# Scores of the second and third transformer layers as row sums on VectorE instead of matmuls on transposed inputs

## The reference, cut to what matters

```python
for l in range(3):
    si = x @ attn_w[l, :256]
    sj = x @ attn_w[l, 256:]
    scores = leaky(si[:, :, None] + sj[:, None, :] + attn_b[l], 0.2)
    attn = softmax(where(mask, scores, -inf))
    h = layernorm(x + attn @ x, g1[l], beta1[l])
    ff = gelu(h @ W1[l] + b1[l]) @ W2[l] + b2[l]
    x = layernorm(h + ff, g2[l], beta2[l])
```

## Time and profile before

| | us |
|---|---|
| median of 3 runs | 3887.73 |
| lowest and highest of them | 3886.62, 3899.89 |
| the profiled execution's own time | 3898.82 |
| its span, first to last instruction | 3896.9 |
| TensorE (PE) busy | 3453.9 |
| VectorE (DVE) busy | 2408.7 |
| ScalarE (ACT) busy | 2204.8 |
| GpSimd (POOL) busy | 695.6 |
| mean granted clock of TensorE | 0.946 of full |

### The profile page before, as it was taken

One profiled execution on the slowest core, in us unless ns is written; L12 is line 12 of the kernel. 1 busy time (PEld: TensorE's weight loads), 2 busy tenths in 40 slices (PEclk: granted clock), 3 DMA queues, 4 the chain that ended last, 5 costly groups with the idle time before them and its releaser, 6 DMA issues.

```text
span 3896.9 us, 60670 instructions
## 1 busy us (share of the span) xinstructions
PE 3453.9 (89%) x18816; PEld 2690.3 (69%) x18816; DVE 2408.7 (62%) x6661; ACT 2204.8 (57%) x4383; POOL 695.6 (18%) x684
## 2 busy tenths in 40 slices
PE   6789989898998989989898898989989899898976
PEld 5667767767777677777777677677767777677653
DVE  3366676666657566676666756566666666766554
ACT  2256556565564746556575564746646565565633
POOL 1211121121212111121121211112121121211110
PEclk8799999999999999999999999999999999999988
DMA  5000000000000000000000000000000000000000
GB/s 129 0 1 12 7 12 7 6 6 6 12 7 6 6 6 12 7 12 6 1 12 7 12 7 6 7 7 12 6 12 7 1 12 6 12 7 1 1 6 6
DMA packets 42354, 39.73 MB, mean 10 GB/s; under 512 B 10017, under 2 KB 40993, under 8 KB 42017
## 3 DMA queue, kind: packets, MB, share of 16 engines
q1 hardware_dynamic: 33568, 27.17, 2.4%
q0 software_dynamic: 8448, 8.39, 1.5%
HBM read 35.55 MB, written 8.39 MB: 11 GB/s over the span
## 4 chain that ended last, share of the span: by engine, by line
PE 48%; issue 33%; DVE 8%; ACT 5%; POOL 5%; DVEq 0%; DMA 0%; POOLq 0%; ACTq 0%; SPq 0%
PE acc L1188 7%; PE work L1174 7%; PE acc L1152 6%; PE work L1097 4%; PE acc L1223 4%; PE acc L1254 3%; POOL rstd L503 3%; PE acc L1235 3%; PE work L1203 2%; PE acc L1283 2%; PE work L1067 2%; PE work L1110 2%; ACT PT L1000 2%; PE work L1235 2%; PE work L1138 1%
## 5 line engine op out<-in xcount | busy, mean ns | idle before, releaser
L1174 PE MATMUL work<-XT,w_sb 128*128 128x256 f32 x3072 | 740.6, 389 | 79.6 <-ACT XT L972 60.9
L503 POOL TENSOR_TENSOR rstd<-var_eps,minus_half 128x2 f32<-128x2 f32 x320 | 233.5, 730 | 3027.9 <-DVE var_eps L727 3027.9
L1188 PE MATMUL acc<-w_sb,gT 128*128 128x256 f32 x3072 | 741.3, 389 | 0.0
L1174 PEld LDWEIGHTS work<-XT,w_sb 128*128 128x128 f32 x3072 | 565.6, 192 | 215.5 <-issue 60.1
L1188 PEld LDWEIGHTS acc<-w_sb,gT 128*128 128x128 f32 x3072 | 588.4, 196 | 101.2 <-issue 22.8
L982 ACT ACTIVATE gT<-work,b_sb 128x256 f32<-128x256 f32 x768 | 346.4, 473 | 227.0 <-PE work L1174 222.5
L1152 PE MATMUL acc<-X,PT 128*128 128x256 f32 x1536 | 359.8, 388 | 32.0 <-ACT PT L950 31.3
L1152 PEld LDWEIGHTS acc<-X,PT 128*128 128x128 f32 x1536 | 292.1, 194 | 86.9 <-issue 48.5
L711 DVE COPY PT<-work 128x512 f32<-128x512 f32 x160 | 110.2, 688 | 237.4 <-PE work L1138 234.7
L718 DVE BATCH_NORM_STATS2 stats<-R 128x6 f32<-128x256 f32 x640 | 240.9, 418 | 11.0
L1152 PE MATMUL acc<-V,PT 128*128 128x256 f32 x1024 | 234.7, 382 | 4.0 <-ACT PT L950 3.8
(11 more groups left out here) (146 smaller groups left out, 6015.0 us busy)
## 6 DMA issues: line engine op xcount, KB each, us to landing
HX<-in_x SPq DMA_DIRECT2D x16, 512.0 KB, 3.9
pos<-in_adj POOLq DMA_DIRECT2D x16, 512.0 KB, 5.5
out<-X SPq DMA_DIRECT2D x32, 256.0 KB, 2.1
w_sb<-in_L_gnn_W SPq DMA_DIRECT2D x6, 1024.0 KB, 7.9
g_sb<-in_L_gnn_g SPq DMA_DIRECT2D x6, 128.0 KB, 4.7
c_sb<-in_L_gnn_beta SPq DMA_DIRECT2D x3, 128.0 KB, 4.3
PT<-in_L_gnn_b SPq DMA_DIRECT2D x3, 128.0 KB, 5.5
beta_sb<-in_L_gnn_beta SPq DMA_DIRECT2D x1, 384.0 KB, 7.7
```

The source lines that it names most:

```text
L503: pool.tensor_tensor(rstd[s][:, half_rows(half)], var_eps[s][:, half_rows(half)], minus_half[:], ALU.pow)\
L1174: last = pe.matmul(u.bank[:, 0:HN], w1_sb[:, l, c, f * P:(f + 1) * P], XT[s][:, c, half * HN:(half + 1) * HN], start=(c == 0), stop=(c == ...
L1188: last = pe.matmul(acc[s][half][:, i, :], gT[s][:, f, i * P:(i + 1) * P], w2_sb[:, l, f, :], start=(f == 0 and i == 0), stop=(f == FC - 1) ...
```

## The change

For L1.1 and L1.2 the stages xT0, xT1 and s are gone. Two new stages, sx0 and sx1, take their place on VectorE: for each of the half's 2 tiles and each of the 2 vectors one instruction multiplies the normalised rows HX element by element with a row of `awr_sb`, writes the products to T (which nothing reads) and adds them up along the row into `s12`, starting from a constant in `ab_sb`. The factor g2 and the shift beta2 of the layer before are folded into `awr_sb` and `ab_sb` once, in the opening. Stage bc on TensorE now waits for all 8 sums. L1.0 keeps its transposes and its stage s. The new list HALF has the same other stages in another order throughout; of it the stretches around the scores are shown, the rest of it is left out.

```diff
-        ("middle", "L1.0", "f210 f211"), ("ending", "L3", "xT0"), ("ending", "L2", "sum1"),
-        ("middle", "L1.1", "xT0"), ("middle", "L1.0", "f212"), ("ending", "L3", "v0"),
-        ("ending", "L2", "norm1"), ("middle", "L1.0", "f213"), ("ending", "L3", "xT1"),
-        ("middle", "L1.0", "xsum1 xnorm1 xa1"), ("ending", "L3", "load qk0"), ("middle", "L1.1", "xT1"),
-        ("ending", "L3", "sq0"), ("middle", "L1.1", "s bc"), ("ending", "L3", "sr0"), ("middle", "L1.1", "zs0"),
...
+        ("middle", "L1.0", "xsum0 xnorm0"), ("ending", "L3", "xT0"), ("middle", "L1.0", "xa0"),
+        ("ending", "L2", "sum1"), ("middle", "L1.0", "f210 f211"), ("ending", "L3", "v0"),
+        ("middle", "L1.1", "sx0"), ("middle", "L1.0", "f212 f213"), ("ending", "L2", "norm1"),
+        ("ending", "L3", "xT1"), ("middle", "L1.0", "xsum1"), ("ending", "L3", "load"),
+        ("middle", "L1.0", "xnorm1 xa1"), ("ending", "L3", "qk0"), ("middle", "L1.1", "sx1"),
+        ("ending", "L3", "sq0 sr0"), ("middle", "L1.1", "bc zs0"), ("ending", "L3", "v1"),
+        ("middle", "L1.1", "mx0 zs1 exp0 mx1"), ("ending", "L3", "qk1"), ("middle", "L1.1", "exp1 pT0 pT1"),
+        ("ending", "L3", "ex0 ex1 sq1 ex2"), ("middle", "L1.1", "agg0"), ("ending", "L3", "ex3 sr1"),
...
+        ("middle", "L1.1", "xnorm1 xa1"), ("ending", "L3", "rr1 rt0 uT28 uT29 uT30 uT31"),
+        ("middle", "L1.2", "sx1"), ("ending", "L3", "rb0 rt1 rb1"), ("middle", "L1.2", "bc zs0"),
+        ("ending", "L3", "hn0"), ("middle", "L1.2", "mx0 zs1"), ("ending", "L3", "proj0 pv3"),
+        ("middle", "L1.2", "exp0 mx1"), ("ending", "L3", "hn1"), ("middle", "L1.2", "exp1 pT0"),
...
-        aw_sb = sb("aw_sb", [P, L, DC, 2])
+
+        aw_sb = sb("aw_sb", [P, DC, 2])
+        awr_sb = sb("awr_sb", [P, L - 1, 2, D])
...
-            uses += [(f"xT0 {k}", DC), (f"xT1 {k}", DC), (f"s {k}", 1), (f"bc {k}", 1), (f"pT {k}", NT)]
+            uses += [(f"xT0 {k}", DC), (f"xT1 {k}", DC), (f"s {k}", 1)] if k == L1K[0] else []
+            uses += [(f"bc {k}", 1), (f"pT {k}", NT)]
...
+        scored = signal("scored", [(k, 2 * NT) for k in L1K[1:]])
...
-        N_LOADS = {"L0": 3, "L2": 2 + 4} | {k: 2 * DC + 1 + 7 + 4 for k in L1K}
-        N_LOADS[L1K[0]] += 1
+        N_LOADS = {"L0": 3, "L2": 2 + 4} | {k: 2 + 5 + 4 for k in L1K}
+        N_LOADS[L1K[0]] += 2 * DC
         N_CONSTS = 8
-        N_FOLDED = {"L0": 2 * DC + 1, "L2": 2 * DC} | {k: 4 for k in L1K}
+        N_FOLDED = {"L0": 2 * DC + 1, "L2": 2 * DC} | {L1K[0]: 4} | {k: 7 for k in L1K[1:]}
...
-                for half in range(2):
-                    for c in range(DC):
-                        load(key, aw_sb[:, l, c, half:half + 1],
-                             attn_w[l, half * D + c * P:half * D + (c + 1) * P].rearrange("(p one) -> p one", one=1))
+                if l == 0:
+                    for half in range(2):
+                        for c in range(DC):
+                            load(key, aw_sb[:, c, half:half + 1],
+                                 attn_w[l, half * D + c * P:half * D + (c + 1) * P].rearrange("(p one) -> p one", one=1))
+                else:
+                    load(key, awr_sb[:, l - 1].rearrange("p k d -> p (k d)"), attn_w[l:l + 1, :].broadcast_to([P, 2 * D]))
...
-                load_columns(key, g2t_sb[:, l], g2[l])
-                load_columns(key, beta2t_sb[:, l], beta2[l])
...
+                        row = awr_sb[:, l - 1]
+                        shifts = PT2[:, 1, 3, 2 * P - 2 * l:2 * P - 2 * l + 2]
+                        dve.tensor_scalar(row[:, 0], row[:, 0], -1.0, None, ALU.mult).then_inc(folded[key], 1)
+                        dve.wait_ge(folded[key], 2)
+                        hold(dve)
+                        for k in range(2):
+                            dve.tensor_tensor_reduce(PT2[:, 2 + k, l - 1, :], row[:, k], beta2_sb[:, l - 1], 1.0, 0.0, ALU.mult, ALU.add,
+                                                     shifts[:, k:k + 1]).then_inc(folded[key], 1)
+                        dve.wait_ge(folded[key], 4)
+                        dve.tensor_tensor(row, row, g2_sb[:, l - 1:l].broadcast_to([P, 2, D]), ALU.mult).then_inc(folded[key], 1)
+                        dve.tensor_tensor(ab_sb[:, l, :, 0], shifts[:, 0:1].broadcast_to([P, NT]), bias, ALU.subtract)\
+                            .then_inc(folded[key], 1)
+                        dve.tensor_copy(ab_sb[:, l, :, 1], shifts[:, 1:2].broadcast_to([P, NT])).then_inc(folded[key], 1)
                     dve.wait_ge(folded[key], N_FOLDED[key])
...
-                    if key in L1K[1:]:
-                        l = L1K.index(key) - 1
-                        dve.tensor_scalar(there, here, g2t_sb[:, l, 1:2], beta2t_sb[:, l, 1:2], ALU.mult, ALU.add)\
-                            .then_inc(u.evacuated, 1)
-                    else:
-                        dve.tensor_copy(there, here).then_inc(u.evacuated, 1)
+                    dve.tensor_copy(there, here).then_inc(u.evacuated, 1)
...
+            def scores_of_rows(half):
+                def stage(s, it, key):
+
+                    l = L1K.index(key)
+                    dve.wait_ge(normed.sems[s], normed.value(it, L1K[l - 1] + " x", half))
+                    hold(dve)
+                    for t in tiles(half):
+                        for k in range(2):
+                            dve.tensor_tensor_reduce(T[s][:, t, k * D:(k + 1) * D], HX[s][:, t, :], awr_sb[:, l - 1, k], 1.0,
+                                                     ab_sb[:, l, t, k:k + 1], ALU.mult, ALU.add, s12[s][:, t, k:k + 1])\
+                                .then_inc(scored.sems[s], 1)
+                return stage
...
-                    if key in L1K[1:]:
-                        l = L1K.index(key) - 1
-                        act.activation(there, here, ACT.Identity, scale=g2t_sb[:, l, 0:1], bias=beta2t_sb[:, l, 0:1])\
-                            .then_inc(u.evacuated, 1)
-                    else:
-                        act.activation(there, here, ACT.Copy).then_inc(u.evacuated, 1)
+                    act.activation(there, here, ACT.Copy).then_inc(u.evacuated, 1)
...
-                    elif key in L1K[1:]:
-                        pe.wait_ge(normed.sems[s], normed.value(it, L1K[L1K.index(key) - 1] + " x", half))
-                        transpose_tiles(s, it, f"xT{half} {key}", HX[s], tiles(half))
...
-                if key in L1K:
+                if key == L1K[0]:
                     u = Use(s, it, f"s {key}")
                     pe.wait_ge(u.evacuated, u.turn + 1)
+                elif key in L1K:
+                    pe.wait_ge(scored.sems[s], scored.value(it, key, 2 * NT - 1))
```

More of the change, by code:

```diff
@@ L181, in build @@
         beta1t_sb = sb("beta1t_sb", [P, L, DC])
-        g2t_sb = sb("g2t_sb", [P, L, DC])
-        beta2t_sb = sb("beta2t_sb", [P, L, DC])
         g1_sb = sb("g1_sb", [P, L, D])
@@ L591, in wait_weights @@
                     dve.tensor_tensor(c1_sb[:, l], c1_sb[:, l], PT2[:, 1, l, 0:D], ALU.add).then_inc(folded[key], 1)
-                    dve.tensor_scalar(aw_sb[:, l, :, 0], aw_sb[:, l, :, 0], -1.0, None, ALU.mult).then_inc(folded[key], 1)
-                    dve.memset(ab_sb[:, l], 0.0).then_inc(folded[key], 1)
-                    dve.wait_ge(folded[key], 3)
-                    dve.tensor_scalar(ab_sb[:, l, :, 0], PT2[:, 1, 3, l:l + 1].broadcast_to([P, NT]), -1.0, None, ALU.mult)\
-                        .then_inc(folded[key], 1)
+                    bias = PT2[:, 1, 3, l:l + 1].broadcast_to([P, NT])
+                    if l == 0:
+                        dve.tensor_scalar(aw_sb[:, :, 0], aw_sb[:, :, 0], -1.0, None, ALU.mult).then_inc(folded[key], 1)
+                        dve.memset(ab_sb[:, l], 0.0).then_inc(folded[key], 1)
+                        dve.wait_ge(folded[key], 3)
+                        dve.tensor_scalar(ab_sb[:, l, :, 0], bias, -1.0, None, ALU.mult).then_inc(folded[key], 1)
+                    else:
+                        row = awr_sb[:, l - 1]
[11 more added lines that the diff above has]
+                        dve.tensor_copy(ab_sb[:, l, :, 1], shifts[:, 1:2].broadcast_to([P, NT])).then_inc(folded[key], 1)
                     dve.wait_ge(folded[key], N_FOLDED[key])
@@ L875, in _ @@
             stages = {"masks": make_masks, "xT": x_transposed(None), "xT0": x_transposed(0), "xT1": x_transposed(1),
-                      "s": scores_of_x, "mx0": leaky_relu(0), "mx1": leaky_relu(1),
+                      "s": scores_of_x, "sx0": scores_of_rows(0), "sx1": scores_of_rows(1), "mx0": leaky_relu(0), "mx1": leaky_relu(1),
                       "sum0": aggregated(0), "sum1": aggregated(1), "norm0": norm(0), "norm1": norm(1),
@@ L1110, in scores_of_x @@
                         last = pe.matmul(u.bank[:, 2 * t:2 * t + 2], XT[s][:, c, t * P:(t + 1) * P],
-                                         aw_sb[:, L1K.index(key), c, :], start=(c == 0), stop=(c == DC - 1))
```

(5 more changed lines are left out.)

## The result

The changed kernel took **3977.38 us** (median of 4 runs, 3970.7 to 3978.74), the kernel before beside it 3890.34: a ratio of 1.0216, with a 95% interval of 1.0194 to 1.0239. It is slower by 2.2%. The forecast said 3776, faster.

The account below looks back on a forecast made before the run. TensorE was taken as the bound, 91% busy where two graphs overlap. A step gains 3.9 + 3.15 - 0.8 + 0.9 = 7.1 us, fifteen 107, with the opening 112: 3787, as a median 3776; range about 3710 to 3880.

Parts of the forecast that it names:

- What VectorE gets: VectorE, per graph: 16 row sums at 0.33 us added, copies and additions removed, net +2.9 us; 0.8 a step exposed.
- signs of being wrong: Half clock behind both broadcasts, waits for line 732 or transpose copies up over 2 us a step, sums much above 0.33.
- L1.1, work on TensorE: Scores of L1.1: first half's transposes give 0.43 us; the broadcast starts at 1033.0 instead of 1035.11, 2.1 us gained.
- L1.1, the clock: Behind L1.1's score matmuls: the half clock goes with them, 1.8 us a step, all of it taken.
- the 3.9 forecast: From qk0 to pv0 at L1.1: 2.1 us from the earlier broadcast and 1.8 us from the clock.
- 0.43 + 0.9 = 1.3 us: L1.2 on TensorE: 0.43 us from the first half's transposes, 0.9 from the small matmul starting earlier.
- half of 2.7: Half clock behind L1.2's scores: 1.9 us at the projection, 0.8 at the small matmul; the middle, 1.35 a step, taken.
- the last ending at 0.50: Row of the last graph's ending: no score matmul runs, yet the clock is 0.50 from 3878.6 to 3885.2 at the projection.
- The new order: The new list puts other work into the waits that arise: 0.9 us a step gained, at most 1.8.
- The opening: First graph alone: shorter latency to the broadcast gives 7.6 us over two layers; less the longer fold, net gain 5.
- The clock still falls: Rival: short waits replace the matmuls and the half clock stays; 3.1 us a step gained, 3837 us, chance 0.21.
- The rival on the slow side: Sums delay VectorE's queue by all 5.3 us, one more clock fall costs 2.7: 4.1 a step lost, 3944, chance 0.07.

Follow-up runs that it names:

- GpSimd late: GpSimd's second-half scaling and X1 shift wait until the next layer's leaky relus are done: sums in old order 3862.94 us, changed kernel 3913.21, kernel before 3924.07.
- GpSimd behind the sums: The changed kernel, with GpSimd's scaling of a half waiting until VectorE has summed that half's rows: 4012.08 us, ratio 1.0306.
- the sums without GpSimd's work: Sums in the old order, GpSimd's scaling and shifting of layer outputs and X1 shift cut to 4 columns: 3833.13 us; kernel before with the same cut 3898.35.

## Why the prediction was wrong

**The step that failed** is "What VectorE gets": "Four row sums at 0.33 us end at 1032.7" and "I take 0.8" for what is exposed. The price was taken from the fold's sums, which run in the opening; it said what a sum costs alone, and not what it costs beside GpSimd. At L1.1 four of them take 5.16 us in the place shown, and TensorE waits 3.56 us for them, where it was to start 2.1 us earlier. Undisturbed they take 1.69 us, for which 1.3 were forecast; a price well above 0.33 us stood among the prediction's own signs of being wrong.

The runs divide the 2.2% into parts, by ratios to the kernel before. The collision costs 1.6% in either order (1.0056 to 1.0216 in the new one, 0.9911 to 1.0069 in the old one), and the new order costs 1.45 or 1.47% with sums (0.9911 to 1.0056 with GpSimd late, 1.0069 to 1.0216 as it was). What is left, the sums in the old order with GpSimd late, is the gain of 0.9%. These three sum to the 2.16% by construction; what supports them is that the collision and the order's price each came out alike on both ways. Neither the gain nor the order's price is clean, though. The gain is measured against a kernel in which GpSimd isn't late; against the matmuls with GpSimd's work in the same place it is 1.5% (late) and 1.7% (left out). And a collision is left in the new order even with GpSimd late, at L1.2 (below).

**The row that would have told it** was in the trace before. Line 651 is a row reduction with both inputs in SBUF, like the new sums, and line 826 the same instruction with one input in PSUM. Durations of line 651 in the kernel before:

```profile
L651 DVE CUSTOM_DVE_ANT_0 T<-T,pos x256: 676/687/1537, 24.7 to 3707.1; 128x512 f32<-128x512 f32 x128
```

And of line 826, the half of it that reads the work banks:

```profile
L826 DVE CUSTOM_DVE_ANT_0 T<-work,pos x128: 685/686/693, 330.3 to 3861.2; 128x512 f32<-128x512 f32 x128
```

The first has a maximum of 1537 over a median of 687, the second varies by 8 ns, and not for want of company: of all 512 instructions of line 826, 98 ran for over 0.3 us beside one of GpSimd's scalings or shifts, and took 681 to 693 ns like the others. A long one of line 651, in the timeline of the kernel before:

```profile
1152.63 1.27 POOL L513 TENSOR_TENSOR R<-R,c_sb 128x512 f32<-128x512 f32 x1
1153.04 1.41 DVE L651 CUSTOM_DVE_ANT_0 T<-T,pos 128x512 f32<-128x512 f32 x1
```

It ends 0.55 us after GpSimd's: most of its own 0.68 comes only then. In the kernel before VectorE's copies for the scores read PSUM (line 627) and took 546 ns at most, 535 in the middle. The change swapped an instruction that no GpSimd instruction stretched for one that it holds, and put it where GpSimd is busy by construction. The Trainium skill says this outright (SBUF — State Buffer, section "SBUF: two separate sides"): VectorE and GpSimd share a port pair as an exclusive lock, held for the whole instruction, and a VectorE instruction with two SBUF inputs needs it against a GpSimd instruction that reads SBUF. The traces agree for GpSimd's scaling and shifting, 0.48 against up to 2.55 us; for its `rstd` instruction, which reads SBUF too, only in part. It gets longer behind a running sum (0.96 us for 0.70), but it is shown as busy beside two further sums and holds neither; there the measurement decides. The prediction weighed the page on the clock and missed this one.

**L1.1, work on TensorE: right when undisturbed.** The forecast was that the broadcast comes 2.1 us earlier; with GpSimd late, in the old order, it came 8.42 - 6.08 = 2.3 earlier. But what follows it gained less: v1 then waited 1.52 us for VectorE's head scores, which is the next thing late. "An engine that waits for something else" had to be asked once more behind the broadcast.

**L1.1, the clock: right in kind.** With the sums undisturbed in the old order, the half clock from qk0 to pv0 is gone (4.9 to 0.0), so it belonged to the score work or to what stood around it; with 2 of the 16 matmuls left it was 2.0. As the change was made, it grew to 8.5, and TensorE's wait of 3.56 us stands ahead of it. In the kernel with GpSimd behind the sums, 5.0 us at half stand ahead of the broadcast, behind a wait of 2.83 us for normalised rows. This much agrees with the Trainium skill (TensorE: Matmul & The Clock Gate, Part 1: The HAM clock gate), by which idle time brings the clock down; that score matmuls with 0.26 us of waiting did the same isn't what it would lead one to expect. But even undisturbed the segment from the broadcast to pv0 is hardly shorter than before (30.84 and 29.86 against 30.20): the 1.8 us did not come through there. The new wait for the head scores takes 1.52 us of them; what takes the rest was not looked for. The mean clock, forecast near 0.955, was 0.938 in the changed kernel and 0.954 with GpSimd late in the old order. From qk0 to pv0 the gain was 1.7 us (GpSimd late) and 2.7 (its work left out) of the 3.9 forecast.

**L1.2: right in its work, wrong in its clock.** 0.43 + 0.9 = 1.3 us were forecast up to the broadcast; from pv0 to it the step became 1.6 shorter with the sums in the old order and GpSimd late. Of the clock I took half of 2.7. At the projection, 1.9 of the 2.7, almost nothing came: it takes 3.78 us as in the earlier trace rows. The small matmul takes 1.12 in place of the 1.70 of the earlier trace rows, but in 8 of 14 steps it took 1.12 before as well, so that its 0.8 was read from one of the slow places. The timeline of TensorE after:

```profile
1379.03 1.12 PE L1292 MATMUL work<-T,head_rows 4*128 4x512 f32 x2 [0.68 <-ACT T L1047]
1380.08 0.95 PE L1143 MATMUL work<-ident,s 128*128 128x128 f32 x4
1381.90 3.78 PE L1300 MATMUL acc<-wo_sb,XT 128*128 128x256 f32 x8 [0.87 <-DVE XT L879]
```

The row that spoke against it, the last ending at 0.50, was the better witness.

**The new order: wrong in sign.** I took 0.9 us a step gained; with the matmuls it costs 1.95, with undisturbed sums 3.4. A part of it is seen: with GpSimd late the first half's sums of L1.2 still took 1.11 and 1.48 us for the first two, as stage sx0 comes closer behind xa0. Another part are TensorE's waits. The two kernels with sums and GpSimd late differ in their order alone; in the old one TensorE waits for normalised rows ahead of its transposes, and for the exponentials ahead of pT:

```profile
PE work L1093 <- DVE X L763: 52.8, 46, 7.9
...
PE work L1163 <- ACT T L968: 19.0, 6, 5.2
```

In the new order:

```profile
PE work L1089 <- DVE X L759: 87.4, 65, 7.9
...
PE work L1159 <- ACT T L964: 50.7, 28, 5.2
```

That is 2.3 and 2.1 us a step more, while the wait of line 1120 for transposed rows (41.5 us in the old order, 9.5 in the new) shrinks by 2.1. So the new order exchanges waits and gains none; no run takes it apart, and the rest stays open.

**The opening: not settled.** Its gain was forecast at 5 us. The first qk0 moved from 321.5 to 321.3 as the change was made, to 317.1 with the sums in the old order, and to 316.6 with GpSimd late besides. So 4.4 of the 5 came in spite of the collision, and the new order took them back; but with GpSimd late the new order had them too (315.3). Each of these is from one execution.

In all, the best undisturbed step is 3.6 us shorter (the sums without GpSimd's work), half of the forecast 7.1. So even without a collision the time is about 3833 (GpSimd's work left out) or 3863 (late), not 3776. The first number is close to the rival "The clock still falls" (3837), but not by its mechanism: at L1.1 the clock did not fall there. The rival on the slow side (3944, measured 3977) had the right kind, blocks of sums that delay VectorE's queue and one more fall of the clock. But it took their 5.3 us from undisturbed sums spread over the step, where the runs show held sums at one place and a price of the new order; that its number is the nearest is in part luck, and it had 0.07.

## What to carry to other kernels

Before an instruction is moved to VectorE, look at where its inputs lie and at what GpSimd does at that time. Take the price of a like instruction with its maximum as well as its median: here a maximum at twice the median, in an instruction that ends just after one of GpSimd's, was the sign of a hold-up, and the like instruction with an input in PSUM was free of it. If GpSimd's result is needed late, let it wait for a point behind VectorE's critical block, and check who stands beside it there, and what stands behind it in GpSimd's own queue. One wait of this kind turned a loss of 0.7% into a gain of 0.9%; one placed earlier turned a loss of 2.2% into 3.1%. And test a new order with the old computation: here it cost 0.8% by itself.

## What was not expected of the hardware

A VectorE row sum of two SBUF operands beside GpSimd's scaling or shift is not slowed in proportion but ends 0.27 to 0.29 us after it: 0.87, 1.47 and 2.55 us for the same 0.47. Beside GpSimd's `rstd` instruction over 128x2, which started after it, the sum takes 0.48, and it is GpSimd's that gets longer: 0.96 us for 0.70 elsewhere, and 0.90 beside the sums with a constant start, which are 0.06 us shorter. Such a sum with its start in a column takes 480 ns where one with a constant takes 421. The clock at L1.1 stood at half behind score matmuls with hardly any wait (0.26 us) and also behind 3.56 us of waiting, and in the old order with neither it stood at full; with 2 of the 16 matmuls left it was at half for 2.0 us a step in place of 4.9. What exactly decides was not settled.
